# Cross-attention scores from four masked key copies, without the way through DRAM, in a new order of the pipeline

## What is computed

```python
# layer 0: cross-attention, 16 heads of 8, 77 context tokens, then a layer norm
scores = einsum('bhqd,bhkd->bhqk', q, k) / sqrt(8)
scores = 0.5 * (scores * mask) + 0.5 * scores     # = scores * wT, wT = 0.5 * mask + 0.5
attn = softmax(clip(scores, -50, 50))
y = layernorm(query + (attn @ v) @ Wo + bo) * gamma + beta
# layer 1: self-attention, 16 heads of 64, in segments of 64 tokens with 17 keys ahead
q, k, v = split(rms_norm(y) @ to_qkv_w); q, k = rope(q), rope(k)
probs = softmax(q @ concat(memory, persistent, k) + causal segment mask)
x = y + (probs @ vf) @ to_out_w
x = x + (silu(g) * a) @ ff_w2 + ff_b2             # a, g = halves of rms_norm(x) @ ff_w1 + ff_b1
```

## Time and profile before

| | us |
|---|---|
| median of 3 executions | 1319.21 (1317.54 to 1330.07) |
| the profiled execution | 1315.27 |
| its span | 1313.5 |
| busy in the span: PE, PEld, DVE, ACT, POOL | 1155.9, 1001.2, 954.3, 1000.9, 997.8 |

### The profile page before, as it was taken

One profiled execution on the slowest core, in us unless ns is written; L12 is line 12 of the kernel. 1 busy time (PEld: TensorE's weight loads), 2 busy tenths in 40 slices (PEclk: granted clock), 3 DMA queues, 4 the chain that ended last, 5 costly groups with the idle time before them and its releaser, 6 DMA issues.

```text
span 1313.5 us, 53289 instructions
## 1 busy us (share of the span) xinstructions
PE 1155.9 (88%) x19811; PEld 1001.2 (76%) x19811; DVE 954.3 (73%) x2511; ACT 1000.9 (76%) x3149; POOL 997.8 (76%) x1678
## 2 busy tenths in 40 slices
PE   0569899999999999999999999999999999999986
PEld 0457788787788878787887878887787878887875
DVE  2446787778777877877787777778778777877772
ACT  1247788888888878788888887888888878888864
POOL 1246788888888888887888888788888888887874
PEclk9978999999999999999999999999999999999999
DMA  6322333333333333334333433333333333334321
GB/s 173 108 82 80 127 120 103 126 124 110 105 129 124 99 121 124 110 109 131 124 108 107 129 122 99 124 124 103 112 125 124 103 122 124 110 108 133 125 78 36
DMA packets 137337, 149.07 MB, mean 113 GB/s; under 512 B 14342, under 2 KB 119707, under 8 KB 137179
## 3 DMA queue, kind: packets, MB, share of 16 engines
q1 hardware_dynamic: 137306, 148.66, 35.6%
HBM read 40.11 MB, written 24.61 MB: 49 GB/s over the span
## 4 chain that ended last, share of the span: by engine, by line
DMA 36%; DVE 24%; PE 21%; SPq 11%; issue 6%; ACT 1%; POOL 1%; DVEq 0%; POOLq 0%; ACTq 0%
DMA qk_dram<-qk_parts 22%; DMA qk_stack<-qk_dram 11%; DVE ra L819 10%; DVE rb L819 10%; SPq L448 5%; SPq L440 5%; PE psum L990 5%; PE psum L1136 3%; PE psum L997 2%; PE psum L983 2%; DVE den L930 2%; PE psum L1017 1%; DMA maskT<-in 1%; PE psum L985 1%; PE psum L984 1%
## 5 line engine op out<-in xcount | busy, mean ns | idle before, releaser
L990 PE MATMUL psum<-xnT,wqkv 128*128 128x128 f32 x2048 | 252.0, 277 | 0.3 <-ACT memT L595 0.3
L990 PEld LDWEIGHTS psum<-xnT,wqkv 128*128 128x128 f32 x2048 | 241.1, 194 | 0.8 <-ACT memT L595 0.5
L516 POOL TENSOR_TENSOR probs_near<-probs,rden 128x256 f32<-128x256 f32 x256 | 158.5, 619 | 93.0 <-DVE rden L937 92.2
L824 DVE TENSOR_TENSOR z<-psum,wT 77x512 f32<-77x512 f32 x256 | 163.7, 679 | 46.6 <-PE psum L997 46.5
L506 POOL TENSOR_TENSOR qT<-ra,rs 128x512 f32<-128x512 f32 x128 | 163.4, 1276 | 34.9 <-DMA rs<-rb 34.9
L819 DVE TENSOR_TENSOR ra<-psum,rope 128x512 f32<-128x512 f32 x256 | 173.4, 677 | 15.0 <-PE psum L990 9.9
L819 DVE TENSOR_TENSOR rb<-psum,rope 128x512 f32<-128x512 f32 x256 | 173.9, 679 | 0.0
L508 POOL TENSOR_TENSOR kall<-ra,rs 128x512 f32<-128x512 f32 x128 | 163.0, 1274 | 5.2 <-DMA rs<-rb 5.2
L512 POOL TENSOR_SCALAR z<-z 77x512 f32<-77x512 f32 x256 | 151.0, 615 | 20.3 <-DVE z L824 19.8
L666 ACT ACTIVATE z<-z 77x512 f32<-77x512 f32 x256 | 148.6, 633 | 15.7 <-POOL z L512 15.5
L829 DVE TENSOR_REDUCE less_max<-psum 128x4 f32<-128x324 f32 x128 | 57.4, 490 | 141.7 <-PE psum L1012 141.7
(11 more groups left out here) (142 smaller groups left out, 3013.4 us busy)
## 6 DMA issues: line engine op xcount, KB each, us to landing
rs<-rb SPq DMA_DIRECT2D x256, 256.0 KB, 2.4
qk_dram<-qk_parts SPq DMA_DIRECT2D x64, 307.5 KB
qk_stack<-qk_dram SPq DMA_DIRECT2D x256, 76.9 KB
vals_far<-vals SPq DMA_DIRECT2D x128, 128.0 KB, 2.4
seq_in<-in SPq DMA_DIRECT2D x64, 166.5 KB
out<-out_sb SPq DMA_DIRECT2D x64, 64.0 KB, 1.8
maskT<-in SPq DMA_DIRECT2D x64, 38.5 KB
ctx_all<-in SPq DMA_DIRECT2D x5, 320.0 KB, 5.6
```

Of the source, the lines that this page charges most:

```text
L516: nc.gpsimd.tensor_tensor(probs_near[:, slots, :], probs[:, slots, 0:SEG], scale.broadcast_to([S, 4, SEG]), ALU.mult)
L824: return V.tensor_tensor(z0[:, 4 * t:4 * t + 4, :], at(f"xs{t}")[0:S2, :].rearrange("k (h q) -> k h q", h=4), wT[:].unsqueeze(1).broadcast ...
L990: last = mm(at(name)[:, S * n:S * (n + 1)], wqkv[:, lo + 128 * n:lo + 128 * (n + 1)], xnT[:], start=n == 0)
```

## The change

- Cross scores: `qk_parts`, `qk_dram`, `qk_stack` and their five DMAs are gone. DVE writes `kz`, four copies of the projected keys in each of which only the rows of every fourth head are kept (`keys_of_heads`, a product with the new columns `own_rows`), and `qb`, the projected queries with their bias. `cross_scores` multiplies row band r (32 partitions) of `kz` copy n with the same band of `qb`, in float32: 16 matmuls as before.
- `v0` is filled by DVE, not ACT.
- Quarters 2 and 3 of the self-attention are like 0 and 1: no `less_maxima`, four exponentials with a bias each.
- All five bodies are in a new order, and PSUM banks and turns of the tasks are given out anew: `gate` moves from `seq[1]` to `seq[2]`, `pv` and `c0T` from `seq[4]` to `seq[5]`, `turned2` from `seq[2]` to `seq[3]`. The memory column `vals_pre` is loaded under `seq[3]`.

```diff
-SHIFTED_BY_PE = (2, 3)
...
+            ("wo", 7, 4, (y_ready,)),
+            ("lin", 6, 1, (sT_ready,)),
+            ("out", 0, 2, (x1_ready,)),
+            ("v1", 6, 3, (vals1_ready,)),
+            ("xs0", 1, 5, (z0_masked,)),
...
+            def keys_of_heads():
+                return V.scalar_tensor_tensor(out=kz[:], in0=at("qkv")[:, S:S + S2].unsqueeze(1).broadcast_to([D, GROUP, S2]),
+                                              scalar=cols[:, BK:BK + 1], in1=own_rows.unsqueeze(2).broadcast_to([D, GROUP, S2]),
+                                              op0=ALU.add, op1=ALU.mult)
...
+                    keys_of_heads()
+                    V.tensor_scalar(qb[:], at("qkv")[:, 0:S], cols[:, BQ:BQ + 1], None, ALU.add).then_inc(qb_ready, 1)
+                    V.tensor_copy(v0[:, :, 0:HD0], at("qkv")[0:S2, 256:384].rearrange("k (h d) -> k h d", h=H)).then_inc(v0_kept, 1)
...
             def cross_scores():
-                for g in range(GROUP):
+                for n in range(GROUP):
                     for r in range(GROUP):
-                        part = slice(32 * r, 32 * r + 3 * HD0)
-                        last = mm(at(f"xs{r}")[0:S2, S * g:S * (g + 1)], qk_stack[part, g, S:S + S2], qk_stack[part, g, 0:S])
+                        rows = slice(32 * r, 32 * (r + 1))
+                        last = mm(at(f"xs{r}")[0:S2, S * n:S * (n + 1)], kz[rows, n, :], qb[rows, :])
                 return last
...
-            def less_maxima(t):
-                return mm(at(f"scores{t}")[:, 0:4 * KEYS].rearrange("i (n k) -> i n k", n=4), ident_b[:],
-                          less_max_b[:, 4 * t:4 * t + 4].unsqueeze(2).broadcast_to([S, 4, KEYS]), start=False)
...
-                    sp.wait_ge(k_rest_ready, done[6])
-                    passed(sp, sp_passed)
-                    sp.dma_start(qk_dram.rearrange("t p s -> p t s"), qk_parts[:, :, 0:S + S2].bitcast(F32)).then_inc(parts_out, 16)
-                    sp.wait_ge(parts_out, done[6] * 16)
```

More of the change, by code:

```diff
@@ new lines, in build @@
+            ("xs1", 0, 5, (z1_masked,)),
+            ("xs2", 3, 5, (z2_masked,)),
+            ("xs3", 4, 5, (z3_masked,)),
+            ("scores2", 5, 3, (probs2_exp,)),
+            ("scores3", 2, 3, (probs3_exp,)),
+            ("v0", 7, 3, (vals0_ready,)),
+            ("xnT", 6, 4, (xnT_ready,)),
+            ("hnT", 4, 2, (hnT_ready,)),
+            ("down", 0, 1, (out_ready,)),
+            ("k0", 6, 4, (k0_rotated,)),
+            ("q0", 2, 4, (q0_rotated,)),
+            ("q1", 0, 4, (q1_rotated,)),
@@ L459, in body @@
                 if seq[3] is not None:
-                    sp.wait_ge(vals0_ready, done[4])
+                    if first(seq[3]):
+                        store_memory_values()
+                    wait(sp, heads_filled, done[3])
                     passed(sp, sp_passed)
-                    for p in range(2):
-                        sp.dma_start(vals_far[SEG * p:SEG * (p + 1), :, :],
-                                     vals[SEG * (1 - p):SEG * (2 - p), :].rearrange("k (a p e) -> k a p e", p=2, e=2 * DH)[:, :, p, :]).then_inc(vals_far_in, 16)
+                    sp.dma_start(vals_pre[0::BAND, :, :].rearrange("n (f h) d -> n f (h d)", f=2),
+                                 memv_dram[bass.ds(seq[3], 1), :].rearrange("b (f n e) -> (b n) f e", f=2, n=4)).then_inc(memv_in, 16)
+                if seq[4] is not None:
+                    if first(seq[4]):
+                        other_weights()
+                    sp.wait_ge(q0_rotated, done[5])
+                    passed(sp, sp_passed)
+                    for odd in range(2):
+                        sp.dma_start(rs[odd::2, half(0)], rb[1 - odd::2, half(0)]).then_inc(swapped0_in, 16)
                 if seq[6] is not None:
+                    if first(seq[5]):
+                        context_loads(2, 3)
+                        first_weights()
+                    wait(sp, qkv_filled, done[6])
                     wait(sp, wT_ready, done[6])
@@ L472, in body @@
                         context_loads(0, 1)
-                if seq[4] is not None:
-                    sp.wait_ge(q0_rotated, done[5])
+                if seq[3] is not None:
+                    sp.wait_ge(vals0_ready, done[4])
                     passed(sp, sp_passed)
-                    for odd in range(2):
-                        sp.dma_start(rs[odd::2, half(0)], rb[1 - odd::2, half(0)]).then_inc(swapped0_in, 16)
+                    for p in range(2):
+                        sp.dma_start(vals_far[SEG * p:SEG * (p + 1), :, :],
+                                     vals[SEG * (1 - p):SEG * (2 - p), :].rearrange("k (a p e) -> k a p e", p=2, e=2 * DH)[:, :, p, :]).then_inc(vals_far_in, 16)
             pipeline(sp, body)
@@ L1002, in weigh_cross @@
                     head = GROUP * g + r
-                    last = mm(at("u")[32 * r:32 * (r + 1), S * g:S * (g + 1)], v0[:, head, :], z0[:, head, :], start=g == 0)
+                    last = mm(at("u")[32 * r:32 * (r + 1), S * g:S * (g + 1)], v0[:, head, :], z0[:, head, :], start=g == 2)
                 return last
```

520 lines of the change are left out of this document (232 added, 288 removed).

## The result

| | before | after |
|---|---|---|
| median of 4 executions, us | 1318.38 (1313.68 to 1330.07) | 1363.6 (1361.12 to 1366.08) |
| span of the profiled execution | 1313.5 | 1364.3 |
| mean granted clock of PE | 0.987 | 0.959 |

The changed kernel is slower by 3.3%: the ratio is 1.0329, with a 95% interval of 1.0259 to 1.0399.

What follows compares the result with a forecast made beforehand. PE, busy 17.63 of 19.03 us a turn, and the loop through DRAM were taken as the bound. The new loop summed to 19.55 or 19.40, taken as 19.45; 64 turns add 27 us to 1319.2: 1346 us, range 1300 to 1372.

Steps and rivals of the forecast that it cites:

- What bounds it before: Loop through DRAM, store to reload: 8.13 us of a 19.03 us turn; PE waits 1.04 a turn for the reload.
- The new loop: From one landing of `vals_far` through PE, DVE and SP's queue to the next: 19.55 us summed, 19.45 a turn taken.
- PE's branch: PE's own order from scores(0) to v1, 3.39 us, instead of DVE's way through the maxima and `through_gate`, 3.54.
- The cross scores: 16 float32 matmuls in row bands on PE: 1.13 us taken, 0.63 more than before.
- The four passes: Rival: float32 cross scores on PE take 2.0 us, 0.87 more a turn than forecast, 1402 us; chance 8%.
- PE's wait: PE waits for `vals_far` at the head of `weigh`, some 1.3 us a turn.
- the first rival: Values land in time and the loop through `maskT` decides: 18.8 us a turn, 1304 us; chance 18%.
- the signs that the prediction gave: In the later profile: 1 to 1.5 us waiting at `weigh`, cross scores 1.0 to 1.3, turns 19.2 to 19.75.
- DVE and ACT at no cost: DVE's added work, about 1.2 us, and ACT's 8 exponentials, under 1.87 us, were both costed at nothing.
- Filling and draining left as they are: The 95 us of the 1313.5 us span outside the 64 turns were taken as unchanged.
- The rival that the values land in time: SP reaches `vals_far` sooner or data land sooner: 18.8 us a turn, 0.23 less than now, 1304 us; chance 18%.
- The rival's floor: PE's work, 17.96 us a turn plus some 0.2 of starts: 0.87 less a turn, 1263 us.

Runs made afterwards that it cites:

- e1: The changed kernel with `vals_far` issued on SP's queue ahead of half 0 of the exchange instead of last: 1292.9 us, ratio 0.9937 to the kernel before.
- e5: The kernel before, in its old order and SP queue, with only the new float32 cross scores without DRAM: 1294.6 us, ratio 0.9958 to the kernel before.
- e4: The changed kernel with `kz`, `qb` and the cross scores' matmuls in float32r: 1312.7 us, ratio 1.0079 to the kernel before.
- e10: The kernel before with only the maxima moved to ACT as bias of the exponentials, no `less_maxima` on PE: 1331.9 us, ratio 1.0289 to the kernel before.
- e9: The changed kernel with `seq_in`, `maskT` and `vals_far` ahead of the exchange, and PE's loop branch put behind queued matmuls: 1230.6 us, ratio 0.9437 to the kernel before.
- e2: The changed kernel with `seq_in`, `maskT` and `vals_far` all issued ahead of half 0 of the exchange: 1261.2 us, ratio 0.9701 to the kernel before.
- e6: The old order with new cross scores, SP's queue alone reordered as in the changed kernel (exchange, `seq_in` with `maskT`, `vals_far`): 1575.6 us, ratio 1.2077 to the kernel before.
- e8: Two kernels: the changed kernel with unused matmuls on PE ahead of the wait for `vals_far` (four, 1342.0 us) or for `maskT` (three, 1331.0 us).

## Why the prediction held, and where it was off

It said slower, 1346 us with a range of 1300 to 1372, and 62% for slower by over 1%. The measured 1363.6 is in the range, 17.6 above the value. The mechanism is the one forecast, as e1 shows: with `vals_far` ahead of the exchange the wait for it is gone, and 4% of the time. That the number came so near is in part luck, as the point on the clock says. By its steps:

- **What bounds it before**, the loop through DRAM: it stands in the trace of the kernel before, where PE waits for it for 1.04 us a turn. Taking it out alone (e5) gains only 6 us: PE's cross scores grow by 0.59 us, and the next loop, through `maskT`, is close. What it was worth in steady turns on the chip of the result isn't measured.
- **The new loop**: right in its members. Measured in the turn of the chain above, with the forecast in brackets: landing to `weigh` 0.13 (0.04); `weigh` 1.79 (1.72); PE's branch from scores(0) to v1 3.59 (3.39, where DVE's of 3.54 was summed); v1 0.92 (0.88); cross scores to DVE 1.18 (1.25); DVE 6.35 (6.38); SP from the rotary's end to the second `vals_far` 3.32 (3.34); its landing 2.46 (2.40). The sum is 19.74, against 19.55 for the worse branch and 19.45 taken. Against PE's branch as forecast (3.39), the largest miss is `wo`: it takes 0.42, where in the timeline of the kernel before L1096 starts 0.23 ahead of the next. Another 0.09 is the time from landing to `weigh`.
- **The cross scores**: 1.09 us against 1.13 taken. The four passes of the Trainium skill (FP8 and Floating Point Precision, TensorE Precision Notes), taken against L997, would have made 2.0, by the prediction's estimate; the trace doesn't agree and decides, with 2.2 times the 0.50 that float32r takes, in L997 and in e4 with the new shape. Their place in the loop was right only for 0.33 of the 0.59 (e4).
- **PE's wait**: forecast as one of 1.3 us at the head of `weigh`. It is two, 0.77 there and 0.85 for `maskT`: the loop through `maskT`, which the first rival names as the next one, was waited for as well. Of the signs that the prediction gave, a wait of 1 to 1.5 us at `weigh` and turns of at most 19.75 are thus missed; undisturbed turns are at that edge, the mean is 20.18.
- **DVE and ACT at no cost**: right, neither appears in the chain for them. Alone in the old order ACT's part does cost (e10), which the prediction didn't say.
- **Filling and draining left as they are**: wrong. Filling fell by 24.5 us, the end rose by 3.1. Some 9 of the 24.5 go already with the way through DRAM (the first `weigh` at 87.6 us in e5); the rest comes with the new order, and what in it brings them stays open.
- **The clock**: not foreseen. The halved clock adds some 0.5 us a turn, about 30 us. This miss and that of filling nearly cancel, which is luck; without both the value would have been 0.3 us a turn, 19 us, too low.
- **The rival that the values land in time**: e1 built it. It takes 19.17, not 18.8. The 0.4 that the two loads ahead might land sooner, because they are small, fits only `maskT` with 38.5 KB; `seq_in` has 166.5, one `vals_far` 128. The rival's floor, PE's own work at 18.2, is reached only with both loads moved and the branch as well (e9, 18.09).

## What to carry to other kernels

On a queue that works in order, a transfer is as late as the latest wait ahead of it. Before a new order of issues is trusted, close each loop from landing to landing and sum it; here moving two blocks of issues ahead was worth 6.5% against the changed kernel (e2), and the changed order of three blocks cost 21% in the old one (e6). When PE becomes the bound, look at where the loop branches, and place the branch behind queued matmuls, not behind a wait that has let the queue run empty.

## What the hardware showed that was not expected

- The branch of a loop on PE costs 0.55 us where the matmul queue is empty (e2), and nothing visible behind 0.9 us of queued matmuls (e9). At one and the same place 0.78 us stand behind it in e2 and 0.2 in e1, where c0, the last thing waited for ahead of it, is ready 1.1 us sooner.
- PE's clock went to half in about a third of the turns of a kernel in which PE is 92% busy (552.97 of 600 us), with two waits of 0.8 us a turn 1.0 us apart. 0.7 to 0.9 us of useless matmuls in either wait kept it at full in the steady turns (e8), and so did 0.6 us less of work elsewhere in the turn (e4).
- 16 float32 matmuls with 32 rows, 77 output rows and 128 columns in four row bands take 1.09 us, 2.2 times the float32r ones, which take 0.50 with 24 rows (L997) and with 32 (e4).
- The kernel before took 1318 us on one chip and 1297 to 1302 on the chips of the experiments, the changed one 1364 and 1362. SP's wait for the store of queries and keys to DRAM is 4.1 us a turn in the first trace (127.4 in 31) and 3.5 on another chip (107.9, e10); that this is all of the difference isn't shown.
